# A fused attention and FFN kernel: the row of maxima reaches the bias row by a 32x32 turning and a small DMA in place of a matmul and a copy

## The reference

```
Q = einsum('bnd,hdk->bhnk', xn, proj_q)      # 8 heads, one K and one V for all
K = einsum('bmd,dk->bmk', xn, proj_k)
V = einsum('bmd,dv->bmv', xn, proj_v)
logits = einsum('bhnk,bmk->bhnm', Q, K)
O = einsum('bhnm,bmv->bhnv', softmax(logits), V)
Y = einsum('bhnv,hdv->bnd', O, proj_o)
ffn = einsum('aemn,enh->amh', einsum('amh,ehn->aemn', xn, w1), w2)
```

## Time and profile before

| | before |
|---|---|
| time, median of 3 runs | 1634.11 us (1634.03 to 1634.44) |
| the profiled execution's own time | 1634.65 us |
| its span, first to last instruction | 1632.9 us |
| PE busy | 1619.3 us, 99% of the span |
| PEld | 1202.5 us, 74% |
| DVE | 1228.6 us, 75% |
| ACT | 1301.2 us, 80% |
| POOL | 1379.2 us, 84% |
| granted TensorE clock | 1.00 |

### The profile page before, as it was taken

The page is one execution under the profiler, slowest core; times in us unless marked ns, Lnnn a source line. Parts: engine busy times, 40 slices in busy tenths (PEclk is TensorE's granted clock), DMA queues, the critical chain, the costliest instruction groups (busy, mean ns, idle before and its releaser), DMA issues. The chain is left out here.

```text
span 1632.9 us, 46345 instructions
## 1 busy us (share of the span) xinstructions
PE 1619.3 (99%) x18710; PEld 1202.5 (74%) x18710; DVE 1228.6 (75%) x2608; ACT 1301.2 (80%) x1349; POOL 1379.2 (84%) x1008
## 2 busy tenths in 40 slices
PE   8999999999999999999999999999999999999998
PEld 6777777777777777777777777777777777777776
DVE  6777777777777777777777777777777777777776
ACT  4688888888888888888888888888888888787786
POOL 3688888888888889888888888888888888888877
PEclk9999999999999999999999999999999999999999
DMA  8000000000000000000000000000000000000000
GB/s 238 4 3 5 5 4 18 4 4 5 3 18 5 4 5 5 16 5 5 4 5 18 3 5 4 4 18 3 5 5 3 18 5 3 4 14 2 2 2 14
DMA packets 34705, 20.41 MB, mean 12 GB/s; under 512 B 18368, under 2 KB 30912, under 8 KB 34496
## 3 DMA queue, kind: packets, MB, share of 16 engines
q1 hardware_dynamic: 33456, 16.92, 3.9%
q10 hardware_dynamic: 1040, 0.52, 0.1%
HBM read 9.57 MB, written 4.19 MB: 8 GB/s over the span
## 5 line engine op out<-in xcount | busy, mean ns | idle before, releaser
L360 POOL TENSOR_TENSOR pr_lo<-pr,pr_hi 128x1024 f16<-128x1024 f32 x511 | 1080.1, 2137 | 227.8 <-ACT pr_hi L463 227.8
L456 ACT ACTIVATE pr<-s_ps,boost,scale 128x1024 f32<-128x1024 f32 x512 | 617.0, 1205 | 193.7 <-PE s_ps L639 193.6
L927 DVE TENSOR_REDUCE key_max<-s_ps 128x128 f16<-128x1024 f32 x512 | 623.9, 1219 | 0.2 <-PE s_ps L624 0.2
L463 ACT ACTIVATE pr_hi<-pr 128x1024 f16<-128x1024 f32 x512 | 525.5, 1051 | 8.1
L637 PE MATMUL s_ps<-g_lo,xT 128*128 128x128 f16 x4096 | 512.4, 219 | 1.0 <-DVE g_lo L940 1.0
L639 PE MATMUL s_ps<-g_hi,xT 128*128 128x128 f16 x4096 | 512.3, 219 | 0.0
L637 PEld LDWEIGHTS s_ps<-g_lo,xT 128*128 128x128 f16 x4096 | 400.7, 98 | 31.4 <-DVE g_lo L940 1.5
L639 PEld LDWEIGHTS s_ps<-g_hi,xT 128*128 128x128 f16 x4096 | 400.8, 98 | 29.9
L679 PE MATMUL t_ps<-pr_hi,xn_hi 128*128 128x512 f16 x1016 | 385.1, 379 | 0.0
L681 PE MATMUL t_ps<-pr_lo,xn_hi 128*128 128x512 f16 x1016 | 385.1, 379 | 0.0
L682 PE MATMUL t_ps<-pr_hi,xn_lo 128*128 128x512 f16 x1016 | 385.1, 379 | 0.0
(11 more groups left out here) (136 smaller groups left out, 1564.1 us busy)
## 6 DMA issues: line engine op xcount, KB each, us to landing
out_dram<-xacc SPq DMA_DIRECT2D x15, 256.0 KB, 2.7
w_sb<-in_L_ffn_w_dram SPq DMA_DIRECT2D x1, 2048.0 KB, 10.0
xT<-xn_hi SPq DMA_TRANSPOSE x56, 2.2
xT<-xn_lo SPq DMA_TRANSPOSE x56, 2.4
pr<-in_L_attn_proj_q_dram ACTq DMA_DIRECT2D x1, 512.0 KB, 4.5
xacc<-in_L_attn_x_dram SPq DMA_DIRECT2D x2, 256.0 KB, 5.1
pr<-in_L_attn_proj_o_dram SPq DMA_DIRECT2D x1, 512.0 KB, 6.7
xacc<-in_L_attn_x_dram SPq DMA_DIRECT2D x1, 384.0 KB, 10.8
```

The source lines that it names most:

```text
L360: pool.tensor_tensor(pr_lo[:, u % RING, :], pr32[:, u % PR, :], pr_hi[:, u % RING, :], ALU.subtract)\
L456: act.activation(pr32[:, u % PR, :], both_banks(u), ACT.Exp, bias=boost[:, 0:1], scale=scale[:, 0:1])\
L463: act.activation(pr_hi[:, u % RING, :], pr32[:, u % PR, :], ACT.Copy).then_inc(p_hi_ready, 1)
L927: dve.tensor_reduce(key_max[:, u % 2, :], both_banks(u).rearrange("p (t q) -> p q t", q=P), AX_X, ALU.max).then_inc(keys_max, 1)
```

## The change

- `max_to_row` and `place_bias` go: no matmul with the identity, no copy into `g_lo` by DVE, and the semaphore `bias_ready` with them.
- `find_max` gets a second DVE instruction: `dve.transpose` of the 128x32 tile `minus_max[:, u % 2, :]` into `max_rows`, in four blocks of 32x32. The 128 maxima then lie in four rows of 32, on partitions 0, 32, 64 and 96. It waits for `find_max`'s own semaphore and for the DMA of unit u-2.
- SP gets `bias(u)`: it waits for the turned rows (`rowed`), for the DMA before, and at j = 0 for `g_lo_ready`, and issues a DMA of four pieces of 64 bytes from those partitions into row 0 of `g_lo`; its end is `bias_in`.
- `low_passes` is split: `low_keys` (x_lo by g_hi, 8 matmuls, waits for `keys_max`) stays about where it was, `low_queries` (x_hi by g_lo, 8 matmuls, waits for `bias_in`) goes to the end of the iteration.
- PE's order within an iteration changes with it, at position 0 and 2 also the places of a chunk's three products.
- DVE: at positions 1, 2 and 3 `between_maxima` comes behind `find_max`; at position 0 it stays ahead of it. ACT: `p_high(n-2)` at position 2 comes ahead of the exponentials.
- SP: the load of 48 tiles of x becomes 24 loads of 2 tiles, one behind each of the bias DMAs of units 6 to 29. The two DMA transposes of a tile are issued behind the bias of two different units, and so are the two stores of a batch.

```diff
-            def place_bias(u):
-                k, j = divmod(u, 4)
-                dve.wait_ge(rowed, u + 1)
-                if j == 0:
-                    dve.wait_ge(g_lo_ready, k + 1)
-                dve.tensor_copy(g_lo[0:1, k % 2, j * P:(j + 1) * P], maxima_row(u)[0:1, :]).then_inc(bias_ready, 1)
+                dve.wait_ge(max_found, u + 1)
+                if u >= 2:
+                    dve.wait_ge(bias_in, 16 * (u - 1))
+                dve.transpose(max_rows[:, u % 2, :], minus_max[:, u % 2, :]).then_inc(rowed, 1)
...
+            def bias(u):
+                k, j = divmod(u, 4)
+                sp.wait_ge(rowed, u + 1)
+                if j == 0:
+                    sp.wait_ge(g_lo_ready, k + 1)
+                if u >= 1:
+                    sp.wait_ge(bias_in, 16 * u)
+                sp.dma_start(g_lo[0:1, k % 2, j * P:(j + 1) * P], max_rows[0:P:Q, u % 2, :]).then_inc(bias_in, 16)
...
+            for u in range(UNITS):
+                bias(u)
+                pair, at = divmod(u, 8)
+                if u in REST:
+                    tile = 2 * NT + 2 * (u - REST[0])
+                    sp.dma_start(xacc[:, tile:tile + 2, :], x_tiles[:, tile:tile + 2, :]).then_inc(x_in[4], 16)
+                if pair == 1 and at in (4, 5, 6, 7):
+                    turn(NT + at // 2 - 2, at % 2)
+                if at in (1, 2) and pair >= 2 and (tile := ln_tile(pair - 2)) is not None:
+                    turn(tile, at - 1)
+                batch = pair // H - 1
+                if pair % H == 2 and at in (5, 6) and batch >= 0:
+                    store(batch, at - 5, 0, HT, 2)
...
             for n in range(UNITS + 3):
                 at = n % 4
                 if n < UNITS:
                     high_pass(n, 0)
-                if 1 <= n <= UNITS and at != 3:
-                    max_to_row(n - 1)
-                if n < UNITS:
                     high_pass(n, 1)
-                if 1 <= n <= UNITS and at == 3:
-                    max_to_row(n - 1)
...
                 chunk(n, 0)
-                small_products(n)
+                if at == 1:
+                    small_products(n)
                 if 1 <= n <= UNITS:
-                    low_passes(n - 1)
+                    low_keys(n - 1)
+                if at != 1:
+                    small_products(n)
                 if at == 2:
-                    chunk(n, 1, rest=False)
+                    chunk(n, 1, (0, 1))
                 if n < UNITS:
                     turn_keys_max(n)
-                chunk(n, 1, first=at != 2)
+                chunk(n, 1, ((0, 1), (0, 1, 2), (2,), (0, 1, 2))[at])
+                if 1 <= n <= UNITS:
+                    low_queries(n - 1)
+                if at == 0:
+                    chunk(n, 1, (2,))
...
                 if n < UNITS:
                     max_of_keys(n)
-                between_maxima(n)
+                if n % 4 == 0:
+                    between_maxima(n)
                 if n < UNITS:
                     find_max(n)
+                if n % 4 != 0:
+                    between_maxima(n)
                 before_bias(n)
```

More of the change, by code:

```diff
@@ L41, in attention_ffn @@
     BANK = 512
+    Q = 32
     SB = 6
@@ L92, in attention_ffn @@
         key_max = sb("key_max", [P, 2, P], F16)
-        minus_max = sb("minus_max", [P, 2, P], F16)
+        minus_max = sb("minus_max", [P, 2, Q], F16)
+        max_rows = sb("max_rows", [P, 2, Q], F16)
         pr32 = sb("pr32", [P, PR, N], F32)
@@ L133, in attention_ffn @@
         g_ps, g_hi_ready, g_lo_ready = sem("g_ps"), sem("g_hi_ready"), sem("g_lo_ready")
-        high_done, keys_max, turned, max_found, rowed, bias_ready = (
-            sem(n) for n in ("high_done", "keys_max", "turned", "max_found", "rowed", "bias_ready"))
+        high_done, keys_max, turned, max_found, rowed, bias_in = (
+            sem(n) for n in ("high_done", "keys_max", "turned", "max_found", "rowed", "bias_in"))
         scores_ready, exp_done, p_hi_ready, p_lo_ready = (
@@ L204, in maxima_turned @@
             return turn_bank(u)[:, 0:P // 2].bitcast(F16)
-        def maxima_row(u):
-            return turn_bank(u + 1)[:, 2 * P:3 * P]
         def ffn_tile(n):
@@ L223, in turned_in @@
             return 32 * (tiles - NT)
+        REST = range(6, 6 + (TILES - 2 * NT) // 2)
         def ln_slot(tile):
@@ L271, in _, with turn @@
             sp.dma_start(w2_sb[:, :, :, :], w2.rearrange("e (c p) d -> p e c d", p=P)).then_inc(w2_in, 16)
-            sp.dma_start(xacc[:, 2 * NT:TILES, :], x_tiles[:, 2 * NT:TILES, :]).then_inc(x_in[4], 16)
-            def turn(tile):
+            def bias(u):
[6 more added lines that the diff above has]
+                sp.dma_start(g_lo[0:1, k % 2, j * P:(j + 1) * P], max_rows[0:P:Q, u % 2, :]).then_inc(bias_in, 16)
+            def turn(tile, half):
                 batch = tile // NT
@@ L278, in turn @@
                 sp.wait_ge(xn_ready, tile + 1)
-                if tile > NT:
-                    sp.wait_ge(xT_in, turned_in(tile))
+                if tile > NT or half > 0:
+                    sp.wait_ge(xT_in, turned_in(tile) + 16 * half)
                 if tile >= KEEP:
@@ L284, in turn @@
                     sp.wait_ge(ffn_ps, tile - KEEP + 1)
-                sp.dma_start(xT[:, 0, at * P:(at + 1) * P], xn_hi[:, at, :], transpose=True).then_inc(xT_in, 16)
-                sp.dma_start(xT[:, 1, at * P:(at + 1) * P], xn_lo[:, at, :], transpose=True).then_inc(xT_in, 16)
+                source = xn_lo if half else xn_hi
+                sp.dma_start(xT[:, half, at * P:(at + 1) * P], source[:, at, :], transpose=True).then_inc(xT_in, 16)
             def store(b, half, first, count, sums):
@@ L488, in _ @@
                     t_high(k - 2)
+                if at == 2 and 2 <= n <= UNITS + 1:
+                    p_high(n - 2)
                 if 1 <= n <= UNITS:
                     exponentials(n - 1)
-                if at == 2 and 2 <= n <= UNITS + 1:
-                    p_high(n - 2)
                 if at != 1 and 1 <= n <= UNITS:
@@ L627, in high_pass, with low_keys, low_queries @@
                     last.then_inc(high_done, 1)
-            def low_passes(u):
+            def low_keys(u):
                 k, j = divmod(u, 4)
-                pe.wait_ge(bias_ready, u + 1)
+                pe.wait_ge(keys_max, u + 1)
+                for t in range(NT):
+                    pe.matmul(bank(u, t // HT)[:, (t % HT) * P:(t % HT + 1) * P], x_lo(batch_tile(k) + t),
+                              g_hi[:, k % 2, j * P:(j + 1) * P], start=False, stop=False, skip_group_check=True)
+            def low_queries(u):
+                k, j = divmod(u, 4)
+                pe.wait_ge(bias_in, 16 * (u + 1))
                 if j == 0:
@@ L635, in low_passes @@
                 for t in range(NT):
[L636 to L640, removed]
+                    last = pe.matmul(bank(u, t // HT)[:, (t % HT) * P:(t % HT + 1) * P], x_hi(batch_tile(k) + t),
+                                     g_lo[:, k % 2, j * P:(j + 1) * P], start=False, stop=True, skip_group_check=True)
                 last.then_inc(scores_ready, 1)
@@ L646, in turn_keys_max @@
                 if u >= 1:
-                    pe.wait_ge(bias_ready, u)
+                    pe.wait_ge(max_found, u)
                 if u == 7:
@@ L651, in turn_keys_max, with weigh @@
                     pe.wait_ge(w1_evacuated, E)
+                if u % 4 == 3 and summing(u - 1) >= 0:
+                    pe.wait_ge(t_lo_ready, summing(u - 1) + 1)
                 pe.transpose(maxima_turned(u), key_max[:, u % 2, :], ident16[:, :]).then_inc(turned, 1)
[L654 to L664, removed]
+            def weigh(k, t, products):
                 tile = (batch_tile(k) + t) % KEEP
@@ L669, in weigh @@
                 dst = sum_bank(k).rearrange("p (j c) -> p j c", j=4)
-                if first:
+                if 0 in products:
                     if t == 0:
@@ L675, in weigh @@
                             pe.wait_ge(t_lo_ready, k - 1)
-                        pe.wait_ge(bias_ready, min(4 * k + 6, UNITS))
+                        pe.wait_ge(max_found, min(4 * k + 6, UNITS))
                         if k == 1:
@@ L679, in weigh @@
                     pe.matmul(dst, xn_hi[:, tile, :], p_hi, start=t == 0, stop=False)
-                if rest:
+                if 1 in products:
                     pe.matmul(dst, xn_hi[:, tile, :], p_lo, start=False, stop=False)
+                if 2 in products:
                     done = pe.matmul(dst, xn_lo[:, tile, :], p_hi, start=False, stop=t == NT - 1)
@@ L694, in weigh_last @@
                 if slot == 0:
-                    pe.wait_ge(bias_ready, UNITS)
+                    pe.wait_ge(max_found, UNITS)
                 for t in (2 * (slot % 4), 2 * (slot % 4) + 1):
@@ L711, in fold_ffn @@
                     pe.wait_ge(max_found, 4)
-                    pe.wait_ge(bias_ready, 3)
                 for c in range(MC):
@@ L717, in fold_ffn, with chunk @@
```

(17 more changed lines are left out.)

## The result

| | before | after |
|---|---|---|
| time, median | 1634.07 us (1633.67 to 1634.44, 4 runs) | 1664.82 us (1664.46 to 1665.18, 4 runs) |
| the profiled execution's own time | 1634.65 us | 1664.77 us |
| its span | 1632.9 us | 1663.0 us |

The ratio is 1.0188, with a 95% interval of 1.0171 to 1.0206: the change makes the kernel slower by 30.7 us, though it makes 512 fewer matmuls. The forecast was 1667 us, slower.

A forecast was written before the change was run, and what follows sets the result against it. PE's own list of matmuls, without gaps, was taken to set the time. 1634.65 - 28.7 + 61 (stalls) + 1 (start and end) = 1668, with the median 0.54 below: 1667 us, range 1630 to 1705.

The forecast's parts named there:

- items 3 and 4: High products at position 2 wait for g_low, at position 0 for the scaling, behind the turning: 0.12 and 0.18 us.
- What goes: 512 matmuls of 0.056 us leave a saturated PE: 28.7 us saved.
- Item 1: turn_keys_max on PE waits for the maximum (L927) at position 3 and every second position 0: 0.05 us per four units.
- Item 2: The projection at position 1 waits for the exponentials of unit n-2: a stall of 0.14 us.
- T: Duration of DVE's turning (128x32, f16, SBUF to SBUF): taken as 0.18 us, bounds 0.08 and 0.28.
- The upper end with 311 ns: The skill's 311 ns as the turning's price would lift its upper end by 0.03 and the sum by some 8 us.
- Item 5: low_queries waits for the bias DMA: taken as 1.8 us, with 2.44 us left at the tightest unit; hidden, 0.
- Sum of stalls: PE's stalls in steady state: 0.49 us per four units, over some 124 blocks, 61 us.
- Start and end: First bias queues behind w2's load, last low pass comes 0.4 us later: 1 us together, between -1 and 3.
- the covers hold: Rival: PE goes on without a gap at all five waits, 1606 us; chance 0.12.
- The DMA takes 2.7 us: Rival: low_queries waits for the bias DMA, some 0.38 us per four units, + 47 us: 1714; chance 0.06.
- the turning waits for POOL: Rival: POOL's subtractions hold the turning, about 0.9 us at positions 1 and 3, near 1890 us; chance 0.02.

The follow-up runs named there:

- c1: Kernel after, with scaling, g_low and t_low ahead of find_max everywhere, two products behind low_queries at position 0, one ahead of the turn at positions 0 and 3: 1611.92 us.
- PE's part of it: c1 with DVE's order as the change has it (find_max ahead of the scaling at positions 1 to 3): 1660.42 us.

## Why the prediction was right

The forecast was 1667 us, measured were 1664.8, inside the range, on the side and for the reasons given. That the two are only 2 us apart is partly luck: the stalls of items 3 and 4 were put 0.12 us per block too high, some 15 us in all, and smaller terms that were too low took most of that back. By its own steps:

- **What goes**, 28.7 us: 27.3 to 27.6 measured where PE is full (the matmul put back).
- **Item 1**, the turn waits for the maximum, 0.05 per block, from 0.03 at position 3 and at every second position 0. The places are right, and an FFN tile covers the wait as foreseen (no gap at 802.71). Each gap is 0.05, so it is 0.07 per block. No run removes this wait alone; it is gone in the two that move a product ahead of the turn, c1 and PE's part of it.
- **Item 2**, the projection waits for the exponentials, 0.14: 0.15, and 19.7 us when it is covered. Right, and the step that rested on no unknown cost.
- **Items 3 and 4**, the high products wait behind g_low and the scaling, 0.12 and 0.18: 0.06 and 0.12. The places are shown by DVE's order as before, the dependence on the turning's length by the turning made twice. The sizes were too large by 0.06 each. T was 0.21, not 0.18; that works against the error. The gap ahead of the turning was 0.04, not 0.11: I had read the 0.11 of the scaling as the price of a second wait, and the turning has a second wait and not that gap. The scaling still has it in the kernel after (the reciprocal ends at 812.90, the scaling starts at 813.01). In the code the scaling waits for its predecessor last and the turning waits for it first; whether this makes the difference wasn't tested. g_low took 0.65 behind the turning, not the 0.69 of the earlier trace rows, and reciprocal to scaling was 0.24, not 0.26. (The upper end with 311 ns would be some 11 us higher and not 8, since T stands in three of its terms; the measured T doesn't need it.)
- **Item 5**, the DMA: hidden, as forecast. Shown by five waits in 512, and by the version that leaves it 1.73 us at unit 1 and where it is late 17 times. The usual landing is thus below the 1.8 that the forecast took. It is also below the 2.0 us that the prediction quotes from the Trainium skill for any DMA: the section named there ("DMA: Bandwidth & Descriptors", "Anatomy of one DMA") gives the figure for DMAs that GpSimd issues, and this one is issued by SP.
- **Sum of stalls**, 0.49 per block. In steady state the kernel after falls behind by what these rows of DVE show, the maxima of units 16 and 504 of before (first two) and after:

```profile
79.65 1.23 DVE L927 TENSOR_REDUCE key_max<-s_ps 128x128 f16<-128x1024 f32 x1
...
1592.70 1.22 DVE L927 TENSOR_REDUCE key_max<-s_ps 128x128 f16<-128x1024 f32 x1
```
```profile
81.59 1.23 DVE L947 TENSOR_REDUCE key_max<-s_ps 128x128 f16<-128x1024 f32 x1 [0.49 <-PE s_ps L642]
...
1622.34 1.23 DVE L947 TENSOR_REDUCE key_max<-s_ps 128x128 f16<-128x1024 f32 x1 [0.49 <-PE s_ps L642]
```

The first pair is 1513.05 us apart, the second 1540.75, for 122 blocks: 27.7 us more, 0.227 per block. With the 4 x 0.056 = 0.224 saved, PE stands still for 0.45 per block. The gaps read above sum to 0.38, or 0.40 with half of the 0.05 at position 0. The rest of 0.05 is in steps of some ten nanoseconds next to these waits: the projection's second product, for instance, starts 0.23 behind its first, where a slot is 0.217. Late DMAs have no part in it, as PE doesn't stand still for one between these units.
- **Start and end**, 1 us: 1.9 behind at unit 16 and 0.5 more at the end, 2.4 in all, at the upper end of what I allowed. In c1 the maximum of unit 16 starts at 80.74, 1.1 behind the kernel before, so some 0.8 of the 1.9 go with the waits that c1 covers. Which step of the start makes the rest wasn't tested.

Of the rivals, "the covers hold" falls for the kernel after, but it marks the place: with the covers lengthened (c1) the time is the 1606 of that case plus 6 us. "The DMA takes 2.7 us" and "the turning waits for POOL" fall: the turning had a median of 0.21 us and a maximum of 0.21 with POOL at work four fifths of the time, as the rule of the Trainium skill ("SBUF — State Buffer", section "Who interferes with whom") has it for a DVE operation with one SBUF input outside the two-port modes.

## What to carry to other kernels

Where one engine is full, an operation taken off it is worth its slot only as long as every wait in the new order is covered; here four places in a block missed by 0.05 to 0.15 us and cost more than 512 matmuls were worth. Moving three products and restoring DVE's order removed these waits, and the kernel came out 22 us faster than before (1611.9 against 1634.1). Check each moved wait by a sum along its chain, from the last start ahead of it to the first start behind it, and put the step that someone waits for ahead of the one that has room: the DMA of the tightest unit had 2.4 us by that sum and mostly needed less than 1.73, the scaling had nothing to spare. PE's drawn busy share hid gaps of up to 0.15 us here, as a matmul is drawn beyond the start of the next one, so count starts per stretch.

## What the runs showed of the hardware

- A bias DMA of four pieces of 64 bytes, SBUF to SBUF, mostly lands within 1.73 us of its issue: with DVE's order as before, unit 1 of each block usually leaves it that (the other units more), and PE's weight loads wait 17 times in 512, up to 0.8 us. Single ones take longer: in c1 the low queries of unit 265, which wait for theirs, start 2.7 us behind its issue. SP's instruction itself is 0.49 us long. The quickest kind in the trace before, 128 KB, took 1.8.
- A 32x32 turning of 128x32 in f16 takes 0.21 us behind find_max and 0.17 behind another turning, and costs DVE 0.13 and 0.10.
- A subtraction of 128x512 from PSUM mostly took 0.65 us where it overlaps the turning ahead of it (kernel after) and 0.69 where DVE stood idle ahead of it (kernel before); I had taken it for fixed.
